# Graph layer on one Trainium2 core: gathered K and V rows of 2048 bytes, V with the head innermost

## The reference

```python
# graph attention: 8 heads of 32; edges e go from src[e] to dst[e], sorted by dst
q, k, v = xn @ Wq.T + bq, xn @ Wk.T + bk, xn @ Wv.T + bv
sim = sum_d(q[dst] * k[src]) / sqrt(32)            # one score per edge and head
p = exp(sim - segment_max(sim, dst)[dst])
agg = segment_sum(p / segment_sum(p, dst)[dst] * v[src], dst)
x = x + agg @ Wo.T + bo + linear_attention(xn)     # 4 heads of 32, 4 memory columns
x = x + mixture_of_8_experts(layernorm(x))         # top 1, capacity 489, 256 -> 1024 -> 256
```

## Time and profile before

| | |
|---|---|
| timed runs, 3, median (lowest to highest) | 1528.84 us (1527.78 to 1534.06) |
| span of the profiled execution, its own time | 1760.6 us |
| edge tables and projection, 0 to about 192 us | DVE busy about half to nine tenths |
| linear attention, 192 to about 270 us | |
| attention, 26 chunks, to 1328 us | DVE six tenths busy |
| output projection and router, to about 1470 us | |
| experts and combine, to the end | PE up to all of the time |

### The profile page before, as it was taken

One profiled execution on the slowest core, in us unless ns is written; L12 is line 12 of the kernel. 1 busy time (PEld: TensorE's weight loads), 2 busy tenths in 40 slices (PEclk: granted clock), 3 DMA queues, 4 the chain that ended last, 5 costly groups with the idle time before them and its releaser, 6 DMA issues. The chain is left out here.

```text
span 1760.6 us, 21501 instructions
## 1 busy us (share of the span) xinstructions
PE 1037.2 (59%) x4059; PEld 679.8 (39%) x4060; DVE 980.2 (56%) x2602; ACT 432.1 (25%) x1253; POOL 536.9 (30%) x608
## 2 busy tenths in 40 slices
PE   0489473555555555455655555555568706999950
PEld 0255342333333333333433333333345704676730
DVE  5479865766666566666666666666687400000017
ACT  1222251222222222222222222222232401212111
POOL 1234434333333343334333333434300060000024
PEclk9999666766666676767677767766669557999985
DMA  4622404333444444434433334444400024424214
GB/s 141 130 73 64 130 1 132 109 109 110 121 117 122 112 129 119 126 109 119 119 114 109 109 114 115 131 120 131 116 25 0 0 70 134 141 83 138 85 36 122
DMA packets 86497, 179.78 MB, mean 102 GB/s; under 512 B 14979, under 2 KB 51909, under 8 KB 86413
## 3 DMA queue, kind: packets, MB, share of 16 engines
q0 software_dynamic: 39872, 117.67, 24.5%
q1 hardware_dynamic: 42125, 57.30, 10.2%
q10 hardware_dynamic: 4416, 4.01, 0.7%
HBM read 157.65 MB, written 21.63 MB: 102 GB/s over the span
## 5 line engine op out<-in xcount | busy, mean ns | idle before, releaser
L1094 PE MATMUL at_pa<-at_pv,at_hot 128*125 128x264 f32 x832 | 326.5, 534 | 247.3 <-DVE agg L973 143.5
L973 DVE TENSOR_TENSOR agg<-agg,at_pa 125x264 f32 x416 | 177.3, 426 | 284.4 <-remote 223.5
L1094 PEld LDWEIGHTS at_pa<-at_pv,at_hot 128*125 128x125 f32 x832 | 193.8, 259 | 340.9 <-issue 282.0
L845 POOL DMA_INDIRECT at_slot<-kv_d,idx x192 | 183.0, 953 | 317.9 <-DVE at_pv L1015 192.0
L845 POOL DMA_INDIRECT slot<-kv_d,idx x192 | 182.9, 953 | 306.4 <-DVE at_pv L1015 165.7
L1039 PE MATMUL at_pq<-q,at_hotT 125*128 x1248 | 217.8, 316 | 38.8 <-DVE agg L1026 22.8
L1039 PEld LDWEIGHTS at_pq<-q,at_hotT 125*128 125x128 bf16 x1248 | 137.0, 111 | 111.8 <-issue 58.9
L1419 DVE TENSOR_TENSOR yb<-xp,b 128x256 f32<-128x256 f32 (+1 forms) x32 | 13.6, 425 | 270.6 <-PE xp L1450 270.6
L902 DVE TENSOR_REDUCE at_sc<-at_prod 128x16 f32<-128x512 f32 x208 | 139.2, 669 | 0.0
L860 ACT ACTIVATE at_habs<-iota_w,nloc_e 128x125 f32<-128x125 f32 x416 | 131.1, 386 | 0.2 <-issue 0.2
L854 ACT ACTIVATE idx<-src_e 128x4 int32 (+1 forms) x100 | 20.5, 205 | 439.1 <-DVE at_pv L1015 418.6
(11 more groups left out here) (295 smaller groups left out, 1408.4 us busy)
## 6 DMA issues: line engine op xcount, KB each, us to landing
w<-in_w SPq DMA_DIRECT2D x16, 1024.0 KB, 7.3
at_locrow<-loc_d SPq DMA_DIRECT2D x26, 500.0 KB
slots_d<-slot SPq DMA_DIRECT2D x7, 512.0 KB
kv_d<-vst SPq DMA_DIRECT2D x25, 128.9 KB
base<-in_x SPq DMA_DIRECT2D x5, 625.0 KB
kv_d<-kst SPq DMA_DIRECT2D x25, 125.0 KB
slot<-kv_d,idx POOLq DMA_INDIRECT x192
at_slot<-kv_d,idx POOLq DMA_INDIRECT x192
```

Source lines behind the costliest of these rows:

```text
L845: pool.indirect_dma_start(slot[par][:, u, :], None, m.kv_d, bass.IndirectOffsetOnAxis(ap=m.idx[:, par, u:u + 1].bitcast(U32), axis=0)).the ...
L973: dve.tensor_tensor(dst, dst, pa[u % 3][:, 0:H * VW].rearrange("p (h c) -> p h c", h=H), ALU.add).then_inc(S.added, 1)
L1094: pe.matmul(pa[u % 3][:, 0:H * VW], hot[:, u % 8, :], pv[:, u % 4, :, :].rearrange("p h c -> p (h c)"), start=True, stop=True).then_inc(S. ...
```

## The change

A gathered row becomes 256 floats of K and 256 of V, 2048 bytes (`KV` = 512). V's columns are ordered d x 8 + h: the weights' third evacuation writes them so, and the bias gets the same order by one DVE copy (`bvp`). The ones are no longer stored and gathered: each row of the two slots is 8 floats longer than what a gather writes (`SW` = 520) and POOL writes ones there once. So `pv`, the PE product and `agg` have the order (33, 8) in place of (8, 33). The scores are ordered step x 8 + head, so `keys` is loaded by 16 DMAs (one per step) to 8 partitions each, where there were 8 to 16 partitions each. The scans over `run` and `runb` still need the head outermost: ACT reads the row of ends in the other order, and the copies to `line` put it back. `norm` writes its result, head outermost, from the head-innermost `agg`.

```diff
-KV = D + H * VW
+KV = 2 * D
+SW = KV + H
@@ edge_tables, scalar, w == 2
+    src = src.rearrange("p i (h d) -> p i h d", h=H)
+    dst = dst.rearrange("p i (d h) -> p i h d", h=H)
@@ project
-        vst = sb("vst", [TT, 2, H, VW])
+        vst = sb("vst", [TT, 2, D])
+        bvp = sb("bvp", [TT, D])
-                for h in range(H):
-                    sp.dma_start(keys[h * U:(h + 1) * U, :, :], bass.AP(m.key.tensor, 0, [[128, U], [U * 128, CH], [1, 130]])).then_inc(S.key_in, 16)
+                for i in range(U):
+                    sp.dma_start(keys[i * H:(i + 1) * H, :, :], bass.AP(m.key.tensor, i * 128, [[0, H], [U * 128, CH], [1, 130]])).then_inc(S.key_in, 16)
-                    sp.dma_start(m.kv_d[rows, D:KV], vst[:, par, :, :].rearrange("p h c -> p (h c)")).then_inc(S.kv_stored[par], 16)
+                    sp.dma_start(m.kv_d[rows, D:KV], vst[:, par, :]).then_inc(S.kv_stored[par], 16)
-                pool.memset(vst[:, :, :, HD:VW], 1.0).then_inc(S.mixv_one, 1)
-                dve.wait_ge(S.key_in, 16 * H)
-                dve.wait_ge(S.mixv_one, 1)
+                dve.wait_ge(S.key_in, 16 * U)
+                dve.tensor_copy(bvp.rearrange("p (d h) -> p d h", h=H), bqkv[:, 2 * D:3 * D].rearrange("p (h d) -> p d h", h=H)).then_inc(S.bv_made, 1)
-                    dve.tensor_tensor(vst[:, par, :, 0:HD], pb[par][:, 0:D].rearrange("p (h d) -> p h d", h=H),
-                                      bqkv[:, 2 * D:3 * D].rearrange("p (h d) -> p h d", h=H), ALU.add).then_inc(S.qkv_out, 1)
+                    dve.tensor_tensor(vst[:, par, :], pb[par][:, 0:D], bvp[:, :], ALU.add).then_inc(S.qkv_out, 1)
+                dve.wait_ge(S.bv_made, 1)
@@ gather_chunk, and the same at L845
-        pool.indirect_dma_start(slot[:, u, :], None, m.kv_d,
+        pool.indirect_dma_start(slot[:, u, 0:KV], None, m.kv_d,
@@ linear_attention, gpsimd, ahead of gather_chunk; attention, gpsimd, ahead of gather_chunk
+                pool.memset(m.slot0[:, :, KV:SW], 1.0)
+                pool.memset(slot[1][:, :, KV:SW], 1.0).then_inc(S.at_const, 1)
@@ attention
-        ph = pp[:, 0:128].rearrange("p (h i) -> p h i", h=H)
+        ph = pp[:, 0:128].rearrange("p (i h) -> p i h", h=H)
-                    act.activation(row[:, :, :, 1:U + 1], pc[0:1, 128:384].rearrange("p (a h i) -> p a h i", a=2, h=H), ACT.Copy).then_inc(S.chain_act, 1)
+                    act.activation(row[:, :, :, 1:U + 1], pc[0:1, 128:384].rearrange("p (a i h) -> p a h i", a=2, h=H), ACT.Copy).then_inc(S.chain_act, 1)
-                    dve.tensor_reduce(sc[:, :, 2 * j:2 * j + 2].rearrange("p h i -> p i h"),
+                    dve.tensor_reduce(sc[:, 2 * j:2 * j + 2, :],
-                        then(dve.tensor_copy(line[:, 0, :, :], run[:, :, 0:U]))
+                        then(dve.tensor_copy(line[:, 0, :, :], run[:, :, 0:U].rearrange("p h i -> p i h")))
-                        then(dve.tensor_copy(line[:, 1, :, :], runb[:, :, 1:U + 1]))
+                        then(dve.tensor_copy(line[:, 1, :, :], runb[:, :, 1:U + 1].rearrange("p h i -> p i h")))
-                        dve.tensor_tensor(scp[:, :, :], sc[:, :, :], spread(at(m.pen_e, n), 1, H), ALU.add).then_inc(S.sc_made, 1)
+                        dve.tensor_tensor(scp[:, :, :], sc[:, :, :], spread(at(m.pen_e, n), 2, H), ALU.add).then_inc(S.sc_made, 1)
-                    dve.tensor_tensor(dst, dst, spread(fac[:, :], 2, VW), ALU.mult).then_inc(S.rescaled, 1)
+                    dve.tensor_tensor(dst, dst, spread(fac[:, :], 1, VW), ALU.mult).then_inc(S.rescaled, 1)
-                        dve.tensor_tensor(pv[:, u % 4, :, :], slot[1 - par][:, u, D:KV].rearrange("p (h c) -> p h c", h=H),
-                                          spread(ph[:, :, u], 2, VW), ALU.mult).then_inc(S.pv_made, 1)
+                        dve.tensor_tensor(pv[:, u % 4, :, :], slot[1 - par][:, u, D:SW].rearrange("p (c h) -> p c h", h=H),
+                                          spread(ph[:, u, :], 1, VW), ALU.mult).then_inc(S.pv_made, 1)
@@ attention_out
-                    dve.tensor_tensor(an[:, par, :].rearrange("p (h d) -> p h d", h=H),
-                                      at(m.agg, t)[:, :, 0:HD],
-                                      spread(at(rden, t), 2, HD), ALU.mult).then_inc(S.an_made, 1)
+                    dve.tensor_tensor(an[:, par, :].rearrange("p (h d) -> p d h", h=H),
+                                      at(m.agg, t)[:, 0:HD, :],
+                                      spread(at(rden, t), 1, HD), ALU.mult).then_inc(S.an_made, 1)
```

More of the change, by code:

```diff
@@ L763, in ps @@
             return ctx.enter_context(nc.psum_tensor("at_" + n, s, F32))
-        slot = [m.slot0, sb("slot1", [128, U, KV])]
+        slot = [m.slot0, sb("slot1", [128, U, SW])]
         locrow = sb("locrow", [TT, U * 128], BF16)
@@ L767, in attention @@
         prod = sb("prod", [128, 2, 2, D])
-        sc = sb("sc", [128, H, U])
-        scp = sb("sc_pen", [128, H, U])
+        sc = sb("sc", [128, U, H])
+        scp = sb("sc_pen", [128, U, H])
         bst = sb("border_st", [128, 2])
@@ L972, in add @@
                     dst = at(m.agg, window)
-                    dve.tensor_tensor(dst, dst, pa[u % 3][:, 0:H * VW].rearrange("p (h c) -> p h c", h=H), ALU.add).then_inc(S.added, 1)
+                    dve.tensor_tensor(dst, dst, pa[u % 3][:, 0:H * VW].rearrange("p (c h) -> p c h", h=H), ALU.add).then_inc(S.added, 1)
                 def body(n, c, nxt, par, turn):
@@ L1025, in _ @@
                 turned_hots(0)
-                dve.memset(m.agg.rearrange("p t h c -> p (t h c)"), 0.0).then_inc(S.at_const, 1)
-                dve.wait_ge(S.at_const, 7)
+                dve.memset(m.agg.rearrange("p t c h -> p (t c h)"), 0.0).then_inc(S.at_const, 1)
+                dve.wait_ge(S.at_const, 8)
                 rounds(dve, body)
@@ L1054, in chain @@
                         pe.wait_ge(S.chain, CHAIN * c + (CARRY_BACK_FLAT if back else CARRY_FLAT))
-                        pe.matmul(pc[:, 384 + back:385 + back], line[:, back].rearrange("p h i -> p (h i)"), one[:, :], start=True, stop=True).then_inc(S.chain_pe, 1)
+                        pe.matmul(pc[:, 384 + back:385 + back], line[:, back].rearrange("p i h -> p (i h)"), one[:, :], start=True, stop=True).then_inc(S.chain_pe, 1)
                     else:
@@ L1079, in body @@
                             pe.wait_ge(S.chain, CHAIN * c + FACTOR)
-                        pe.transpose(scT, scp[:, :, :].rearrange("p h i -> p (h i)"), m.ident[:, :]).then_inc(S.sc_turned, 1)
+                        pe.transpose(scT, scp[:, :, :].rearrange("p i h -> p (i h)"), m.ident[:, :]).then_inc(S.sc_turned, 1)
                     if c is None:
@@ L1144, in _ @@
                 st = m.dve_steps.on(dve)
-                st.link(dve.tensor_scalar(rden[:, :, :], m.agg[:, :, :, HD], 0.5, None, ALU.max))
+                st.link(dve.tensor_scalar(rden[:, :, :], m.agg[:, :, HD, :], 0.5, None, ALU.max))
                 st.link(dve.reciprocal(rden[:, :, :], rden[:, :, :]))
@@ L1530 @@
 SEMS = """dve_step xr_made qr_made hr_made edges_in tbl_const last_in keys_out keys_made tbl_iota ident_zero ident_made
-rows_known before_made rows_counted tbl_turned w_in b_in bo_in zero_made zero_out qkv_out mixv_one squared base_x
+rows_known before_made rows_counted tbl_turned w_in b_in bo_in zero_made zero_out qkv_out bv_made squared base_x
 var_made std_made xn_made w_ready ss_made norm_made rms_made projected w_turned w_evac xn_turned xnT_made mix_out
@@ L1548, in __init__ @@
          self.before_made, self.rows_counted, self.tbl_turned, self.w_in, self.b_in, self.bo_in, self.zero_made,
-         self.zero_out, self.qkv_out, self.mixv_one, self.squared, self.base_x, self.var_made, self.std_made,
+         self.zero_out, self.qkv_out, self.bv_made, self.squared, self.base_x, self.var_made, self.std_made,
          self.xn_made, self.w_ready, self.ss_made, self.norm_made, self.rms_made, self.projected, self.w_turned,
@@ L1667, in graph_layer @@
                 linear_attention(nc, m, io)
-            m.agg = att.enter_context(nc.sbuf_tensor("agg", [TT, NT, H, VW], F32))
+            m.agg = att.enter_context(nc.sbuf_tensor("agg", [TT, NT, VW, H], F32))
             attention(nc, m)
```

15 lines of the change are left out of this document (8 added, 7 removed).

## The result

The changed kernel takes 1546.47 us (median of 4 runs, 1541.69 to 1546.67); the kernel before took 1528.31 us (4 runs, 1524.9 to 1534.06) beside it. The ratio is 1.011 with an interval of [1.0086, 1.0134]: slower by 1.1%, some 17 us, where 1555 us had been forecast. Its profiled execution has a span of 1544.9 us, close to its timed runs.

What follows compares the result with a forecast made beforehand. The prediction saw a row of stages, with DVE bounding attention. Keys 13.5, copies 7.7, norm 4.1 and weight evacuation 0.3 made 25.6 us on top of 1528.84, say 1555 us; range 1541 to 1570.

Steps and rivals of the forecast that it cites:

- The 13.5 us: Key loads ahead of the projection: 8 partitions per DMA use fewer DMA engines, so DVE starts later; +13.5 us, bounds 0 and +14.
- Rival A: Key loads use all 16 DMA engines after all, so they get no longer: +12 us, 1541 us; chance 14%.
- The statement that nothing behind makes it up: Projection behind the keys: its tiles keep their pace, so the shift of 13.5 us is passed on whole.
- whole: Norm of the output projection (L1151), writing in steps of 32 words: +163 ns, 25 times, all counted; +4.1 us.
- The copies to the line: Attention's 52 copies (L927, L946), reading in steps of 17 words: +149 ns each, +7.7 us, counted whole.
- The prediction's own sign: Copy to the line at L946: 290 to 370 ns if the forecast is right, still 214 ns if steps are free.
- rival B: Steps of several words are free in such short DVE operations: +13.5 us, about 1543 us; chance 10%.
- (c): ScalarE reading the chain's row in attention in steps of 8 words: taken as 0, range 0 to 4.2 us.
- 9 us are free: GpSimd in attention: gathers need 20.1 us of a chunk of about 29 us, so 9 us are slack covering them.
- each used a chunk later: Attention's gathers: a distance of one chunk between issue and use, so their change costs or gains nothing.
- Rival C: Gathers matter: aligned 2048-byte rows shorten DVE's waits at the additions behind them, giving 1503 us; chance 10%.
- The remote waits: DVE's 223.5 us of waits at attention's additions (L973): taken as something only the profiled execution has, absent from timed runs.

Runs made afterwards that it cites:

- e1: The kernel before, unchanged, timed and profiled again: 1527.39 us, ratio 0.9995.
- e3: The kernel before with only its keys, in their old order, loaded by 16 DMAs to 8 partitions each: 1538.73 us, ratio 1.0067.
- e2: The changed kernel with its keys loaded by 8 DMAs to 16 partitions each, 8 apart: 1532.87 us, ratio 1.0028 to the kernel before.
- e5: The kernel before with only the two copies to the line reading in steps of 17 words: 1529.18 us, ratio 1.0008.
- e10: The kernel before with DVE's bias copy and its wait added ahead of the projection's loop, result unused: 1536.39 us, ratio 1.0055.
- e4: The kernel before with only the norm writing its 256 elements in steps of 8 words: 1531.94 us, ratio 1.0026.
- e7: The kernel before without the last 4 of 16 gathers of each chunk and their waits: 1503.95 us, ratio 0.9856.
- e8: The kernel before with indices staged and gathers released after every 2 pv in place of 4: 1520.32 us, ratio 0.9955.
- e6: The kernel before gathering only K, in rows of 1024 bytes: 1772.65 us, ratio 1.0018, where the kernel before takes 1769 us.
- e9: The changed kernel, keys by 8 DMAs to 16 partitions, gathers released per 2 pv, where the kernel before takes 1769 us: 1813.72 us, ratio 1.0255.
- e11: The kernel before with 64 empty DVE instructions ahead of attention: 1767.97 us, ratio 0.9996, where the kernel before takes 1769 us.
- e12: The same kernel as e9, run where the kernel before takes 1526 us: 1520.71 us, ratio 0.9965.

## Why the prediction came out as it did

Time and direction were right: 1546.47 us lies in the range, slower by over 0.5%. The sum forecast 25.6 us and 17 came, and it came in other parts than the text says.

*The keys: right in us.* The 13.5 us rested on a number of engines per DMA, which was the author's estimate; no run shows it. What the runs show in its place is the share and the wait: with 8 partitions per DMA the DMA share is half (0.63 for 1.25). The wait grew by 12.3 us (28.7 less 16.38) where 13.5 was taken, and DVE began 10.9 us later than in e1. e3 gives +10.2 us [7.0, 13.3] for this edit by itself, e2 the way back. Rival A, in which the load gets no longer, falls. The issue costs more per DMA than before, 19.74 us for 16 where 8 took 5.36, but it is over nearly 9 us before DVE goes on. The statement that nothing behind makes it up holds up to linear attention (+11.2); the 3.6 us less after it are the clock's, as e5 and e10 show.

*The norm: right, though hardly "whole".* 4.1 us were taken, e4 measures +4.0 [1.8, 6.1], and in the changed kernel the norm takes 592 ns where 420 + 163 = 583 was forecast. PE's wait for it grew from 6.0 us to 8.1. In the profiles the stage grew by 2.6 us for 4.4 us of longer instructions.

*The copies to the line: wrong.* 7.7 us were taken, and e5 finds +1.2 us with no change inside its interval [-1.1, +3.7]. The step that failed is the price of 1.24 ns per element, carried from a reduction of 3200 elements that steps by 512 bytes. A step of 17 words costs 40 ns for 128 elements by the medians (214 and 254 ns), 0.3 ns each; 52 copies make 2.1 us. The prediction's own sign was 290 to 370 ns. Here rival B was right. With all that they take, 254 ns for 128 elements are 2.0 ns each, the norm's 592 ns for 256 are 2.3; the step adds 0.3 ns per element to the copies and 0.67 to the norm.

*The terms taken as nothing or nearly so: right.* The value products take 420 ns where e1 has 422, ScalarE reads the chain's row in 373 ns in both kernels, so (c) adds nothing. The third weight evacuation takes 1089 ns where it took 597, 0.5 us once in place of 0.3.

*The turns of attention's loop: missing from the sum.* The bias copy and its wait were put down as free since the wait for the keys covers them. It does cover their own time. But with them every turn of attention's loop takes longer: chunks with the jump 32.30 us in place of 31.60, attention +7.6 us, and e10 gives +8.4 us [5.3, 11.6] for these two instructions alone. Two thirds of it lie at two fixed places of DVE's list away from the jump, a smaller part in the pause at the jump itself. No view of before pointed there, since this price lies in no instruction's own duration.

Keys, norm and turns by their own experiments add up to 22.6 us, 23.8 with the copies, and the change costs 16.8 [13.1, 20.5]. Each has an interval of 2 to 3 us to either side, so the sums fit at best at the edge; whether the parts overlap by a few us is open. In the forecast the copies' 7.7 us stood where the turns' 7.6 us belong. That was luck, and part of why the total came near.

*"9 us are free" and "each used a chunk later": wrong, without harm to the number.* The rows are those of the next chunk, but its products run in the same chunk of time, behind the last `pv`. So the burst of gathers lies in the circle, as e7 and e8 show. It did no harm because 32 bytes less change nothing that can be seen: the gathers take 954 ns where they took 953, and with half the bytes 953 (e6). Rival C was right that the gathers matter and wrong in how: no faster addition came of the new rows. Their number (e7) and their start (e8) count. The idle time of GpSimd was read as slack though its releaser row named `pv`.

*The remote waits: an error of inference.* They were taken as a thing of the profiled execution alone. But e1 has none while profiled. Beside e6, e9 and e11 the kernel before takes 1769 us in plain timed runs, and the profiles of these three show the waits. So they belong to the chip, or to that session on it, and not to the profiler. The estimate of 29 us for a chunk built on it was near all the same: 30.2 and 31.6.

## What to carry to other kernels

Look at how many partitions each part gets before splitting a load that an engine waits for: with 16 DMAs to 8 partitions each DVE waited 28.7 and 29.0 us for the keys, with 8 DMAs to 16 it waited 16.9 (e1) and, the partitions 8 apart, 11.8 (e2). Idle time of an engine is slack only if it may work in it: draw the circle from release to use before calling it free, and shorten the release (here -0.5%). When an edit costs more than its parts, compare the turns of a loop step by step with those of before, over all turns: two instructions ahead of a loop made pauses at fixed places inside it, and a single turn pointed at the wrong place.

## What the runs showed of the hardware

- Eight DMAs to 16 partitions each load the same 1.73 MB faster if the partitions are 8 apart: a wait of 11.8 us (12.7 in e12) in place of 16.9 in e1 and 16.4 to 18.8 in the other runs with 16 neighbouring ones. The source is read alike, and while only keys move the DMA share is the same (1.23 and 1.25), but 193 GB/s arrive in place of 120. Why is open.
- At the jump of attention's loop DVE stands still for 2.8 to 4.1 us between the last addition and the first product (e1 2.9 to 3.9). With two more instructions ahead of the loop, two fixed places inside it take 0.38 and 0.17 us longer in every turn.
- The same kernel takes 1526 to 1528 us on three chips and 1769 us on a fourth, there steady within 10 us (1763.68 to 1772.83). On the fourth 219 to 229 us of waits without a visible source stand at the additions, in attention only, whatever the bytes per row or 64 instructions ahead. What they are no run here settles, nor whether they are the chip's or that session's.
- In linear attention's tiles the granted clock of TensorE differs between executions for no reason in the edit: 0.50 to 0.57 in e1, e4 and e8 (35.2 to 35.3 us), 0.81 to 0.86 in the changed kernel, e3, e5 and e10 (31.4 to 32.6 us).
- A ScalarE copy of 1 x 256 elements takes 373 ns whether it reads them in steps of 8 words or not (L883, L876). One of 128 x 512 elements that writes in steps of 8 words takes 1089 ns in place of 597 (L326, L321).
